# A conditioned transformer block on one core: start-up work spread anew, and the first quarter's projections in full float32

## The reference

```
x  = x + causal convolution of x along the tokens, 32 lags, weight cond[lag, channel] (depthwise)
ada = cond @ ada_w + ada_b      -> shift1, scale1, gate1, shift2, scale2, gate2
x1 = layernorm(x) * (1 + scale1) + shift1
q, k, v = x1 @ qkv_w + qkv_b    (16 heads of 128)
a  = softmax(q k^T / sqrt(128)) v,  within each sequence of 32
r  = x + gate1 * (a @ out_w + out_b)
h  = gelu((layernorm(r) * (1 + scale2) + shift2) @ ffn_w1 + ffn_b1)
out = x + (r + gate2 * (h @ ffn_w2 + ffn_b2))
```

## Time and profile before

| | |
|---|---|
| median of 3 runs | 339.06 us (336.91 to 346.12) |
| profiled execution | 337.3 us, span 335.5 us |
| mean granted PE clock | 0.964 |
| PE busy | 311.0 us (93%) |
| DVE, ACT, POOL busy | 181.7, 166.5, 128.7 us |
| chain that ended last | PE 69%, DVE 19%, ACT 6% |

### The profile page before, as it was taken

How to read it: one execution, slowest core, us unless ns; L and a number is a source line. 1 busy time by engine, 2 the same in 40 slices (tenths; PEclk the granted TensorE clock), 3 DMA queues, 4 the chain that set the end, 5 groups by cost and what they waited for, 6 DMA issues and landing times.

```text
span 335.5 us, 6092 instructions
## 1 busy us (share of the span) xinstructions
PE 311.0 (93%) x2587; PEld 261.1 (78%) x2587; DVE 181.7 (54%) x299; ACT 166.5 (50%) x298; POOL 128.7 (38%) x113
## 2 busy tenths in 40 slices
PE   4977899499999959999999999999999998999994
PEld 3876899388888847887888788788888887678884
DVE  2995635606796994635543653743342164747232
ACT  6231545542764524537627563762862785533910
POOL 6830902630780453109307411830930761620400
PEclk9997699789999996999999999999999999999999
DMA  7920210350062062003402500430340200000011
GB/s 231 339 65 0 70 59 0 90 165 0 2 189 63 0 189 63 2 1 127 127 0 71 180 4 2 134 118 0 124 130 2 64 0 0 2 1 0 2 63 63
DMA packets 14987, 23.00 MB, mean 69 GB/s; under 512 B 776, under 2 KB 8048, under 8 KB 14960
## 3 DMA queue, kind: packets, MB, share of 16 engines
q1 hardware_dynamic: 14912, 22.58, 21.4%
q10 hardware_dynamic: 48, 0.03, 0.0%
HBM read 21.57 MB, written 1.05 MB: 67 GB/s over the span
## 4 chain that ended last, share of the span: by engine, by line
PE 69%; DVE 19%; ACT 6%; issue 3%; POOL 1%; DMA 1%; DVEq 0%; ACTq 0%; POOLq 0%
PE bank L830 16%; PE bank L831 15%; PE bank L832 15%; DVE xc L485 11%; PE bank L902 8%; PE bank L791 2%; PE bank L838 2%; PE bank L840 2%; PE bank L839 2%; PE bank L888 2%; DVE x1l L544 2%; ACT wh L321 2%; PE bank L816 1%; DVE sd L565 1%; PE bank L823 1%
## 5 line engine op out<-in xcount | busy, mean ns | idle before, releaser
L267 POOL TENSOR_TENSOR wl<-raw,wh 128x512 fp32r<-128x512 f32 x72 | 99.3, 1410 | 134.0 <-ACT wh L321 134.0
L830 PE MATMUL bank<-x1h,wl 128*128 128x512 f32 (+1 forms) x176 | 70.6, 401 | 8.9 <-POOL wl L267 4.7
L364 ACT ACTIVATE pool<-bank,bT 128x512 f32<-128x512 f32 x56 | 38.5, 687 | 62.6 <-PE bank L832 62.6
L831 PE MATMUL bank<-x1l,wh 128*128 128x512 f32 (+1 forms) x176 | 67.7, 385 | 0.0
L832 PE MATMUL bank<-x1h,wh 128*128 128x512 f32 (+1 forms) x176 | 67.5, 383 | 0.0
L485 DVE SCALAR_TENSOR_TENSOR xc<-x,condT,xc 128x496 f32<-128x496 f32 (+30 forms) x86 | 49.8, 652 | 0.1
L591 DVE SCALAR_TENSOR_TENSOR ol<-bank,bT,oh 128x512 fp32r<-128x512 f32 x32 | 23.8, 749 | 46.1 <-ACT oh L389 45.2
L830 PEld LDWEIGHTS bank<-x1h,wl 128*128 128x128 f32 x176 | 35.1, 200 | 16.9 <-POOL wl L267 6.0
L321 ACT ACTIVATE wh<-raw 128x512 fp32r<-128x512 f32 x72 | 40.9, 625 | 3.5 <-PE bank L832 3.5
L831 PEld LDWEIGHTS bank<-x1l,wh 128*128 128x128 f32 x176 | 35.2, 200 | 6.2 <-issue 0.7
L832 PEld LDWEIGHTS bank<-x1h,wh 128*128 128x128 f32 x176 | 35.1, 199 | 6.3
(11 more groups left out here) (102 smaller groups left out, 423.6 us busy)
## 6 DMA issues: line engine op xcount, KB each, us to landing
raw<-in_L_cond_qkv_w_dram SPq DMA_DIRECT2D x24, 512.0 KB, 3.9
raw<-in_L_cond_out_w_dram SPq DMA_DIRECT2D x8, 512.0 KB, 4.2
raw<-in_L_cond_ffn_w_dram SPq DMA_DIRECT2D x4, 512.0 KB, 3.5
adaw<-in_L_cond_ada_w_dram SPq DMA_DIRECT2D x1, 1024.0 KB, 10.7
out_dram<-pool SPq DMA_DIRECT2D x4, 256.0 KB, 2.2
pool<-in_x_dram SPq DMA_DIRECT2D x2, 256.0 KB, 3.1
adaw<-in_L_cond_ada_w_dram SPq DMA_DIRECT2D x1, 512.0 KB, 4.9
pool<-in_x_dram SPq DMA_DIRECT2D x1, 512.0 KB, 8.1
```

What stands on the lines that cost most here:

```text
L267: g.tensor_tensor(wl[:, cols], raw[:, cols], wh[:, cols].bitcast(F32), ALU.subtract)\
L364: a.activation((q_sb if j < GH else k_sb)[:, j % GH, :], src, ACT.Identity, bias=bias(U, j // GH, j % GH)).then_inc(s_ev, 1)
L830: pe.matmul(dst, wl[:, w_cols], a_hi, start=start, stop=False)
L831: pe.matmul(dst, wh[:, w_cols], a_lo, start=False, stop=False)
```

## The change

It consists of these parts.

- `PE_BOTH` begins at lag 11: PE does 21 lags and VectorE 11. The diagonals are shared anew: ScalarE makes those of the first channels and every second one of the others (31), GpSimd the remaining 11. VectorE copies one more piece of x out of PSUM in ScalarE's place.
- The semaphores of the weights' high and low parts are split in four (q, k, v, output), so the pieces can be made in another order on GpSimd than they lie in memory. GpSimd makes its first low parts only when the first quarter's convolution is summed.
- The first quarter's projections (`project_first`) read x1 and `raw` directly, in full float32, and wait neither for x1's high and low parts nor for the weights'. In return, unit 1's loads into `raw` wait for these projections.
- PE's order: `mean(0)` ahead of `modulation(0)`; the transposes of x's second half and `modulation(1)` ahead of the first projections; `var(1)` and `spread(1)` between them. The banks of the modulation and of the transposes change, and VectorE takes parts 1 and 2 of the modulation together.
- ScalarE and GpSimd make the weights' parts in another order: in unit U first q of U+1 (behind `o_high(U-1, 2)`), then k, then the output weights of U, then v. `exps(U)` and x1's high parts stand earlier in ScalarE's queue.
- VectorE's second-half convolution: two lags ahead of the low parts of the attention's output and single lags between them.

```
@@ constants
-    PE_BOTH = list(range(13, 32))
-    DVE_LAGS = [list(range(13)), list(range(T))]
+    PE_BOTH = list(range(11, 32))
+    DVE_LAGS = [list(range(11)), list(range(T))]
+    BY_ACT = [(d, ct) for d in range(len(DIAG_LAGS)) for ct in range(CT) if ct == 0 or d % 2]
+    BY_POOL = [(d, 1) for d in range(0, len(DIAG_LAGS), 2)]
...
-        ADA_BANKS = [PB[0], YB[0], YB[1]]
+        ADA_BANKS = [PB[0][:, 0:ADA1 * B], OB[1][:, 0:ADA1 * B], OB[1][:, ADA1 * B:2 * ADA1 * B]]
@@ SyncE
             def load_qkv(U, i):
                 if U:
-                    sp.wait_ge(s_wlo, 8 * (U - 1) + 2 * i + 2)
+                    sp.wait_ge(s_wlo[i], 2 * U)
+                if U == 1:
+                    sp.wait_ge(s_proj, 2 * i + 2)
@@ GpSimd
+            def low_part(U, p):
+                i, cols = p // 2, slice(PIECE * p, PIECE * (p + 1))
+                g.wait_ge(s_whi[i], 2 * U + p % 2 + 1)
+                g.tensor_tensor(wl[:, cols], raw[:, cols], wh[:, cols].bitcast(F32), ALU.subtract)\
+                    .then_inc(s_wlo[i], 1)
...
-            low_parts(0, range(0, 2))
+            g.wait_ge(s_in, CT)
+            low_parts(0, 0)
+            low_part(0, 2)
             rstd(0)
+            low_part(0, 3)
+            g.wait_ge(s_x1f, CT)
+            low_part(0, 4)
             rstd(1)
-            g.wait_ge(s_lo, CT)
-            low_parts(0, range(2, 6))
+            low_part(0, 5)
             g.memset(pt[:, :, :, :], 0.0).then_inc(s_zero, 1)
-            low_parts(0, range(6, 8))
-            low_parts(1, range(0, 6))
+            low_parts(0, 3)
+            for i in range(3):
+                low_parts(1, i)
             for U in range(1, NU):
...
-                low_parts(U, range(6, 8))
-                low_parts(U + 1, range(0, 6))
+                low_parts(U + 1, 0)
+                low_parts(U + 1, 1)
+                low_parts(U, 3)
+                low_parts(U + 1, 2)
@@ ScalarE
-            diagonals(14, len(DIAG_LAGS))
-            high_parts(0, range(0, 4))
+            for i in range(3):
+                high_parts(0, i)
...
+            for ct in range(CT):
+                a.wait_ge(s_xt, 3 + ct)
+                a.activation(half(x0, ct, 1), YB[ct][:, :], ACT.Copy).then_inc(s_xe[2], 1)
+            evac_chunk(0)
+            evac_chunk(1)
             x1_high(0)
-            high_parts(0, range(4, 6))
+            evac_chunk(2)
             x1_high(1)
-            for j in range(UB):
+            for j in range(3, UB):
                 if j == UB - 1:
                     exps(0)
                 evac_chunk(j)
...
+                if j == 6:
+                    high_parts(0, 3)
                 if j == 8:
-                    high_parts(0, range(6, 8))
-            high_parts(1, range(0, 6))
+                    high_parts(1, 0)
+                if j == 10:
+                    high_parts(1, 1)
+            high_parts(1, 2)
...
                 o_high(U - 1, 2)
+                high_parts(U + 1, 0)
                 o_high(U - 1, 3)
-                evac(U, 5)
-                high_parts(U, range(6, 8))
-                evac(U, 6)
-                high_parts(U + 1, range(0, 2))
-                evac(U, 7)
...
+                for j in (5, 6, 7, 8):
+                    evac(U, j)
+                high_parts(U + 1, 1)
                 exps(U)
-                for j in (9, 10, 11):
-                    evac(U, j)
-                high_parts(U + 1, range(4, 6))
+                evac(U, 9)
+                high_parts(U, 3)
+                evac(U, 10)
+                evac(U, 11)
+                high_parts(U + 1, 2)
@@ VectorE
-            v.wait_ge(s_xe[2], CT)
-            conv(1, 0, 2)
             modulation(1)
             modulation(2)
             one_plus(2, SCALE2)
-            conv(1, 2, 5)
+            v.wait_ge(s_xe[2], CT)
+            conv(1, 0, 5)
             softmax_front(0)
...
-            for h in range(GH):
-                o_low(0, h)
-            conv(1, 5, 13)
+            conv(1, 5, 7)
+            o_low(0, 0)
+            o_low(0, 1)
+            conv(1, 7, 8)
+            o_low(0, 2)
+            conv(1, 8, 9)
+            o_low(0, 3)
+            conv(1, 9, 17)
@@ TensorE
+            def project_first(tiles):
+                t0, nt = CHUNKS[0]
+                for i in tiles:
+                    if i % 2 == 0:
+                        pe.wait_ge(s_raw[i // 2], 16)
+                    if i >= 3:
+                        pe.wait_ge(s_ev, i - 2)
+                    if i < 4:
+                        for h in range(2):
+                            for kt in range(CT):
+                                c0 = 1024 * (i // 2) + PIECE * kt + P * (2 * (i % 2) + h)
+                                m = pe.matmul(PB[i % 3][:, nt * h:nt * (h + 1)], raw[:, c0:c0 + P], ln_c(0, kt),
+                                              start=(kt == 0), stop=(kt == CT - 1))
+                    else:
+                        for kt in range(CT):
+                            m = pe.matmul(PB[i % 3][:, :], ln_c(0, kt)[:, P * (i - 4):P * (i - 3)],
+                                          raw[:, 2048 + PIECE * kt:2048 + PIECE * (kt + 1)],
+                                          start=(kt == 0), stop=(kt == CT - 1))
+                    m.then_inc(s_proj, 1)
...
+            conv_both(14, len(PE_BOTH))
+            mean(0)
             pe.wait_ge(s_adaw[0], 16)
             modulation(0)
-            mean(0)
+            var(0)
             mean(1)
-            var(0)
             spread(0)
-            var(1)
-            spread(1)
...
-            project_chunk(0, range(0, 6))
             pe.wait_ge(s_x[2], 16)
...
             pe.wait_ge(s_adaw[1], 16)
             modulation(1)
+            pe.wait_ge(s_x1f, CT)
+            pe.wait_ge(s_adat, 2)
+            project_first((0,))
+            var(1)
+            project_first((1, 2))
+            spread(1)
+            project_first((3, 4, 5))
             modulation(2)
             pe.wait_ge(s_lo, CT * 2)
             project_chunk(1, range(0, 5))
```

More of the change, by code:

```diff
@@ L209, in load_out @@
                 if U:
-                    sp.wait_ge(s_wlo, 8 * U)
+                    sp.wait_ge(s_wlo[3], 2 * U)
                 r0 = (U % NG) * PIECE
@@ L298, in _ @@
                 hidden_low(0, m)
-            low_parts(NU, range(6, 8))
+            low_parts(NU, 3)
             for m in (4, 6):
@@ L308, in _, with high_parts, diagonals @@
             a.dma_start(crow[:, :], cond).then_inc(s_row[0], 16)
-            def high_parts(U, pieces):
-                for p in pieces:
-                    cols = slice(PIECE * p, PIECE * (p + 1))
-                    if p % 2 == 0:
-                        a.wait_ge(s_raw[p // 2], 16 * (U + 1))
-                        if U:
-                            if p < 6:
-                                a.wait_ge(s_proj, UB * (U - 1) + 4 * (p // 2 + 1))
-                            else:
-                                a.wait_ge(s_y, CT * U)
-                    a.activation(wh[:, cols], raw[:, cols], ACT.Copy).then_inc(s_whi, 1)
-            def diagonals(d0, d1):
-                for d in range(d0, d1):
+            def high_parts(U, i):
+                a.wait_ge(s_raw[i], 16 * (U + 1))
+                if U and i < 3:
+                    a.wait_ge(s_proj, UB * (U - 1) + (4 * (i + 1) if U > 1 else 6 + 2 * (i + 1)))
+                elif U:
+                    a.wait_ge(s_y, CT * U)
+                for p in (2 * i, 2 * i + 1):
+                    cols = slice(PIECE * p, PIECE * (p + 1))
+                    a.activation(wh[:, cols], raw[:, cols], ACT.Copy).then_inc(s_whi[i], 1)
+            def diagonals(n0, n1):
+                for d, ct in BY_ACT[n0:n1]:
                     j = DIAG_LAGS[d]
-                    a.activation(diag[:, CT * d, :], ident[:, :], ACT.Copy,
-                                 scale=condT[:, 0, T - 1 - j:T - j]).then_inc(s_diag[0], 1)
+                    a.activation(diag[:, CT * d + ct, :], ident[:, :], ACT.Copy,
+                                 scale=condT[:, ct, T - 1 - j:T - j]).then_inc(s_diag[0], 1)
             a.wait_ge(s_const, 3)
@@ L333, in _ @@
             diagonals(0, 2)
-            a.wait_ge(s_xt, 1)
-            a.activation(part(x0, 1, CHUNKS[0]), OB[1][:, 0:256], ACT.Copy).then_inc(s_xe[1], 1)
-            a.wait_ge(s_xt, 2)
-            for ct in range(CT):
-                a.activation(part(x0, ct, CHUNKS[1]), YB[ct][:, 0:256], ACT.Copy)\
-                    .then_inc(s_xe[1], 1)
-            diagonals(2, 14)
+            for n in range(2):
+                a.wait_ge(s_xt, n + 1)
+                a.activation(part(x0, 1, CHUNKS[n]), (OB, YB)[n][1][:, 0:256], ACT.Copy).then_inc(s_xe[1], 1)
+            diagonals(2, len(BY_ACT))
             a.wait_ge(s_bt, 1)
             a.activation(bT[:, :], PB[2][:, 0:NBIAS], ACT.Copy).then_inc(s_btc, 1)
-            diagonals(14, len(DIAG_LAGS))
-            high_parts(0, range(0, 4))
+            for i in range(3):
```

(20 more changed lines are left out.)

73 lines of the change are left out of this document (34 added, 39 removed).

## The result

The changed kernel takes 326.94 us (median of 4 runs, 326.39 to 327.69) against 339.36 us (336.91 to 346.12) for the kernel before beside it: a ratio of 0.9638, with a 95% interval of 0.9569 to 0.9708. It is faster by 3.6%, and the time lies in the range 317 to 330 but 4.4 us above the 322.5 forecast. The profiled execution took 327.43 us for a span of 325.6 us, 9.9 less than the 335.5 of before; the sum had promised 14.7 less.

What follows compares the result with a forecast made beforehand. The prediction took the kernel as bound by PE, with start-up holes each paid again as a half-clock stretch. Its terms summed to -14.7, giving 320.8 us of span and, with 1.8 outside it, 322.5 us; range 317 to 330.

Steps and rivals of the forecast that it cites:

- Step 1: First-half convolution: PE takes lags 11 and 12, VectorE ends near 20, mean at 23.7 instead of 25.44, -1.7.
- Steps 2 and 3: First quarter's norm and float32 projections: first projection at 32.0 instead of 35.86, second quarter at 45.5 instead of 50.2, -4.7.
- step 2: Norm of the first quarter, at full clock: first projection starts at 32.0 instead of 35.86.
- The sum's own slow bound for the three steps: Start-up to the second quarter: if the clock drops in 29 to 36, the gain is -1.3 instead of -4.7.
- Step 4: PE's wait for weights, 60.4 to 65.08, goes: -4.7, and -2.2 from 11 slow matmuls behind it.
- the waits of step 5 drop the clock: Rival at the first softmax: PE's waits bring slow clock, 2.8 us more, 325.3; chance 0.17.
- step 6: PE's wait at 121.9, third softmax, goes: -3.6, and -2.8 from 14 slow matmuls; bounds 0 and -6.4.
- Step 5: First softmax: ten VectorE steps take four turns with GpSimd pieces; PE waits 1.55 and 2.35, +3.9.
- the rival in which VectorE keeps going: First softmax: VectorE keeps the port beside GpSimd's pieces, no wait added, 318.6; chance 0.22.
- The bound of 0 from 86.1 to 89.2: First softmax's low bound: no loss, as VectorE kept full pace there while GpSimd's piece stood still.
- Step 7: Later units: two other waits behind ScalarE's copies go, as copies of q and x1 come earlier, -0.6.
- the rival on the slow side: Later units: ScalarE stands at the next q's copy until its load lands, 351 us; chance 0.05.

Runs made afterwards that it cites:

- e7: Changed kernel with GpSimd writing zeros, reading nothing, for low parts of unit 0's output weights and unit 1's q, k, v: 320.81 us, ratio 0.944.
- e3: Changed kernel with the first half's convolution split as before (PE lags 13 to 31, VectorE 0 to 12): 329.7 us, ratio 0.9576 resting on two of four runs.
- c1: The changed kernel run once more, nothing altered: 327.35 us, ratio 0.9651.
- e1: Changed kernel with four of VectorE's ten convolution steps ahead of the first softmax put behind it: 321.21 us, ratio 0.9439.
- e4: Kernel before with only VectorE's new order of second-half convolution against the attention output's low parts: 336.85 us, ratio 0.9692 resting on three of 11 runs.
- e6: Changed kernel with PE's first-half convolution lags in the order 11 to 16, then 31 down to 17: 323.28 us, ratio 0.9495.
- after: The changed kernel itself in its first profile, against the kernel before: median 326.94 us, ratio 0.9638; profiled execution 327.43 us.
- e5: Changed kernel with PE's first-half convolution lags in the order 11, then 31 down to 12, narrow products first: 327.86 us, ratio 0.9614.
- e2: Changed kernel with the first quarter's projections in three passes from high and low parts again: 325.74 us, ratio 0.9578.
- e10: Changed kernel with fewer VectorE steps ahead of the first softmax, convolution split at lag 13 and three-pass first quarter: 322.05 us, ratio 0.9453.

## Why the prediction was right or wrong

The direction and the range were right, and the gains that came stand where the sum had put them. That the time fell within the range isn't the same as a right sum: two clock terms were missed, both on the slow side, and the rest hit or came a little better. The profile of the changed kernel holds 5.8 us of shortfall in these two terms.

**Step 1 was right.** VectorE's share ended at 19.8 (near 20 in the forecast) and PE set the end, 0.6 us of waiting. PE came 0.8 us sooner, at 22.2 for 23.0, as the clock's first rise stood at 9.34 instead of 11.76; in e7, with the rise at 11.89, its part ended at 23.5. But e3 shows the gain over 25.44 was not the split's: with lags 11 and 12 back on VectorE the mean starts at 22.24. What is left of what the step named is that GpSimd's low pieces no longer run beside the steps; that was not run by itself.

**Steps 2 and 3: the failed term is the clock of step 2.** The forecast took full clock "since PE pauses 0.7 and 0.8 us only", from a stretch at 1.00 with the same kinds of instructions. PE paused 0.6 us, and the clock was at half for 10.2 us. Sixteen modulation records cost 3.46 instead of 1.8, the variance 1.84 instead of 0.95, the second mean 2.05; the first projection starts at 35.23 for 32.0, all of the 3.2 missing. The quarter itself was sized right: 35.23 to 48.70 is 13.5, as 32.0 to 45.5. The sum's own slow bound for the three steps, -1.3, was met almost exactly (-1.5). By the Trainium skill's rule (TensorE: Matmul & The Clock Gate, Part 4: PE-mode transpose), that transposes don't count as PE being busy, this step would also be at -1.3. The size agrees, the mechanism is not what the rows show: the clock fell at 23.0, nine microseconds ahead of the transposes at 32.10, and rose at 33.2, while they ran. What the runs show in place of the pauses that the sum weighed is that the same start-up, with the same 0.6 us of pause, falls at 23.0, 27.6 or 29.0 (c1, e7).

**Step 4.** The wait for weights went, -4.9 for -4.7. The 2.2 us of slow matmuls did not come back, since a new hole takes the place of the old one and has its own slow stretch: 12 matmuls at 0.43 us, for 11 before. That is the rival "the waits of step 5 drop the clock", put at 2.8 and 0.17; it happened, and e1 removes both parts. I had expected two short holes (1.55 and 2.35) and so judged the clock safe; it was one of 3.18. Two products of the sum are also rounded up: 11 x 0.19 is 2.1, not 2.2, and 14 x 0.19 in step 6 is 2.7, not 2.8.

**Step 5: the size was near (+3.2 for +3.9), by two errors that cancel.** Six pieces came beside the ten steps, not four, so VectorE ended at 62.26, 4.9 us after the scores were ready instead of 3.0, and PE stood 3.2 instead of 1.55. The second hole, 2.35, did not open: VectorE's transposes were done at 69.0, and PE, whose own tiles ran at half clock meanwhile, came to them at 70.08. At full clock it would have come some 2.4 sooner and waited about 1.3 (an estimate from these rows). The mechanism (turns of about 1.05 us a piece, against the rival in which VectorE keeps going) is shown by e7: VectorE lost a full 1.03 for each piece. The bound of 0 from 86.1 to 89.2 was not met.

**Step 6 was right**, -6.0 for -6.4, with 3.34 us to spare for VectorE where I had counted 2.5; e4's trace shows it by itself, 7.2 in the same measure. **Step 7** was -1.1 for -0.6. ScalarE's copy of the next q held up nothing in units 2 to 7: the rival on the slow side did not occur.

**Open.** What sets the clock's first rise, and with it the moment at which it falls between 23 and 38 us: the same start-up gave three answers. Whether float32 or three passes is better to less than 1 us once e1's order is in, and whether e6's order does anything, are hidden by the same spread.

## What to carry to other kernels

Count the GpSimd pieces that fall beside a VectorE stretch with two SBUF inputs before placing that stretch on a path: here each cost 1.03 us, and moving four of ten steps to the other side of the softmax was worth 5.7 us, beside the 12.4 of the whole change. Price a hole of 3 us in TensorE with the half-clock stretch behind it (2.4 us here), and check that no new hole opens close to a removed one: here the one at 61.6 took back what the one at 60.4 had given. In a ragged start-up, carry the slow clock as a bound of the forecast or as its centre; and test the edit that a change is named after alone, since here it gained nothing in this change as it stands and probably cost about 1 us, while its companions brought the gain.

## What the runs showed of the hardware that was not expected

In this kernel the clock stayed at half for 10.2 us while PE was busy all the time and had paused for 0.6 us only (after, 23.0 to 33.2), and the place differs between executions of one start-up (27.6 to 37.8 in c1, 29.0 to 32.4 in e7). In all twelve profiles of the changed kernel and its variants the clock falls once or twice between 23 and 37 us; early first rises (9.3 to 9.7) went with the long stretch, later ones (11.9 to 12.0) with the short one. Narrow products at the head of PE's queue went with a first rise at 16.92 (e5).

The same wait of 3.2 us at the first softmax was followed by 6.8 us at half clock in four profiles (after, c1, e3, e5) and by 3.4 us in two (e2, e6). A hole of 1.9 us (e10, 193.3 to 195.2) was followed by none: the clock there stays at 1.00.

PE can stop for 3.28 us within a run of 128 equal small products, with no semaphore and no other engine involved (e4, 207.2 to 210.4); e10's hole of 1.9 us stands within such scores too. The traffic of the kernel's own loads can't be the common cause: the DMA share is 0.63 in the first and 0.00 in the second. A 16 KB load of the instruction queue ran close to both (at 207.8 and at 192.6), but each execution has twenty such loads, and the other nineteen pass without a hole. That PE had run out of instructions fits this but is only argued. Such a hole with a slow stretch behind it might also be why e3's runs fall into two groups about 7 us apart; no run of the longer group was profiled.
